# A selective-scan and expert-choice kernel: a reordered prologue, X loaded in one go, and a copy moved to ScalarE

## What is computed

```python
x = x + _layernorm(mamba(_layernorm(x)))
x = x + _layernorm(experts(_layernorm(x)))
# mamba: u, z = split(x @ in_proj);  u = silu(conv1d(u) + conv_b)
#   delta, b, c = split(u @ x_proj);  delta = softplus(delta @ dt_proj + dt_b)
#   h = exp(delta * a) * h + delta * b * u  over 256 steps, 256 channels x 16 states
#   y = (einsum(h, c) + u * D) * silu(z);  return y @ out_proj
# experts: scores = softmax(h @ gate_w.T); each of 16 experts takes its 32 best tokens
#   of a sequence, gated MLP (gelu), scattered back; plus a shared gated MLP
```

## Time and profile of the kernel before

| | us |
|---|---|
| median of 3 runs (1392.88 to 1401.41) | 1394.62 |
| the profiled execution | 1400.59 |
| its span, first to last instruction | 1398.9 |
| first product on GpSimd | 63.42 |
| first scan on VectorE | 65.87 |
| last work of the Mamba block | 908.2 |
| expert block, first part | 908.6 to about 1050 |

### The profile page before, as it was taken

One profiled execution on the slowest core, in us unless ns is written; L12 is line 12 of the kernel. 1 busy time (PEld: TensorE's weight loads), 2 busy tenths in 40 slices (PEclk: granted clock), 3 DMA queues, 4 the chain that ended last, 5 costly groups with the idle time before them and its releaser, 6 DMA issues. The chain is left out here.

```text
span 1398.9 us, 15385 instructions
## 1 busy us (share of the span) xinstructions
PE 1094.9 (78%) x4128; PEld 510.1 (36%) x4128; DVE 1103.3 (79%) x1440; ACT 889.4 (64%) x1614; POOL 938.9 (67%) x503
## 2 busy tenths in 40 slices
PE   4667878787777878777777876445998989999796
PEld 2322222222222222222222322133755336666695
DVE  7499999999999999999999999896382962222288
ACT  3567577667667677667667665356332866666796
POOL 0199999999999999999999999722010740000176
PEclk9878899989999899989998898867798999999898
DMA  5745835834834835834834836110000001111013
GB/s 159 152 101 112 183 71 111 182 81 101 182 77 105 182 75 107 182 85 97 182 81 101 183 81 162 41 31 1 1 0 23 1 1 34 44 35 34 12 31 91
DMA packets 48490, 122.87 MB, mean 88 GB/s; under 512 B 5824, under 2 KB 20928, under 8 KB 42304
## 3 DMA queue, kind: packets, MB, share of 16 engines
q1 hardware_dynamic: 46864, 121.01, 39.1%
q10 hardware_dynamic: 1584, 1.36, 0.3%
HBM read 83.55 MB, written 5.24 MB: 63 GB/s over the span
## 5 line engine op out<-in xcount | busy, mean ns | idle before, releaser
L555 POOL TENSOR_TENSOR states<-b_dup,dup 128x1024 f32<-128x1024 f32 x256 | 596.5, 2359 | 63.3 <-DMA dup<-dd 61.7
L648 DVE TENSOR_TENSOR_SCAN da<-da,states 128x1024 f32<-128x1024 f32 x160 | 359.5, 2283 | 38.7 <-ACT da L397 32.6
L397 ACT ACTIVATE da<-dup,decay 128x510 f32<-128x510 f32 x512 | 327.2, 672 | 11.1 <-DVE states L648 11.1
L295 PE MATMUL yp<-states,fold 128*64 128x512 f32 x1024 | 275.4, 664 | 15.6 <-DVE states L574 9.8
L534 POOL TENSOR_TENSOR states<-states,X 128x1024 f32<-128x1024 f32 x96 | 226.1, 2356 | 20.5 <-DVE states L648 20.4
L648 DVE TENSOR_TENSOR_SCAN states<-da,states 128x1024 f32<-128x1024 f32 x96 | 218.7, 2278 | 7.0 <-ACT da L397 7.0
L574 DVE TENSOR_TENSOR states<-da,X 128x1024 f32<-128x1024 f32 x160 | 192.5, 1203 | 0.0
L1664 POOL TENSOR_SCALAR put<-row_t,slot_i,slot_w 128x256 f32<-128x256 f32 x32 | 39.1, 1222 | 193.3 <-POOLq L1368 173.5
L393 ACT ACTIVATE da<-zeros 128x4 f32<-128x4 f32 x177 | 30.5, 173 | 197.2 <-DVE states L574 196.3
L295 PEld LDWEIGHTS yp<-states,fold 128*64 128x64 f32 x1024 | 69.4, 152 | 212.5 <-issue 196.2
L1469 DVE TENSOR_TENSOR hx<-glx,upx 128x512 f32<-128x512 f32 x64 | 41.3, 684 | 126.6 <-ACT glx L1434 118.2
(11 more groups left out here) (185 smaller groups left out, 1779.9 us busy)
## 6 DMA issues: line engine op xcount, KB each, us to landing
b_dup<-bc_rows SPq DMA_DIRECT2D x32, 1024.0 KB, 9.6
dup<-dd SPq DMA_DIRECT2D x128, 256.0 KB, 11.7
X<-bc_rows SPq DMA_DIRECT2D x64, 512.0 KB, 11.5
out<-X SPq DMA_DIRECT2D x3, 1024.0 KB, 5.1
wg<-in_wgT SPq DMA_DIRECT2D x16, 128.0 KB, 2.1
wu<-in_wuT SPq DMA_DIRECT2D x16, 128.0 KB, 2.2
wd<-in_wdT SPq DMA_DIRECT2D x16, 128.0 KB, 2.2
bc_rows<-bcf SPq DMA_DIRECT2D x16, 64.0 KB, 1.6
```

Source lines behind the costliest of these rows:

```text
L295: last = nc.tensor.matmul(yp[64 * i:64 * i + 64, :], fold[:], states[:, (2 * step + i) % RING, s, :], start=False, stop=(q == 3 and s == S ...
L397: ins = nc.scalar.activation(factors[:, s, :].rearrange("p (b t) -> p b t", b=2)[:, :, 1:S], src[:, :, 1:S], ACT.Exp, scale=decay[:, col:c ...
L555: nc.gpsimd.tensor_tensor(states[:, i % RING], b_dup[:, par, s0:s0 + SPI, :], dup[:, par, 1, h, g, :].unsqueeze(1).broadcast_to([P, SPI, N ...
L648: nc.vector.tensor_tensor_scan(to.rearrange("p s t -> p (s t)"), factors.rearrange("p s t -> p (s t)"), ring.rearrange("p s t -> p (s t)") ...
```

## The change

- SP asks for X in four parts of 4, 28, 16 and 16 tiles (`X_PARTS`), all at the start, without the wait for the weights. ScalarE issues `conv_w` first, and loads its tables ahead of their use (`preload_act_table_set`, `preload_act_table`).
- Only pair 0 goes through statistics, `inverse` and `norm` before the first projection. Pair 1 follows inside the softplus, the others behind it. The statistics of tiles 32 to 47 and 48 to 63 move behind the softplus' last VectorE step.
- The first nine projections alternate between two PSUM banks (`bank`): one waits for the evacuation of the last but one. `wp` moves ahead of CONV0, BC ahead of DELTA0. The softplus of pair 0 runs by channel halves (`log_half`, `lost_half`, `softplus_half`, `inputs_half`), and `whole_banks` fills its two PSUM banks with a matmul at the start.
- The norms of pairs 12 to 15 are done by ScalarE (`normalised`, with `shift` = -mean * rstd).
- In pair 0 SP sends both halves of delta and delta * u before c; GpSimd starts only when VectorE has done all its norms (`xh_ready` 48).
- `take_logits` is done by ScalarE, the first copy at n = 8 behind `turned`, the second at the end.

```diff
+        X_PARTS = ((0, CH), (CH, 2 * QT), (2 * QT, 3 * QT), (3 * QT, TILES))
-        BEFORE = (CONV0, CONV1, DELTA0, DELTA1, BC, Z0, Z1)
+        BEFORE = (CONV0, CONV1, BC, DELTA0, DELTA1, Z0, Z1)
+        def bank(no):
+            return yp if isinstance(no, int) and no < len(BEFORE) + 2 and no % 2 else mp
...
-                if not (isinstance(no, int) and no == 0):
+                if not (isinstance(no, int) and no < len(BEFORE) + 2):
                     pe.wait_ge(mp_free, no)
+                elif no > 1:
+                    pe.wait_ge(mp_free, no - 1)
... TensorE
             pe.wait_ge(id_ready, 1)
-            turn(0)
+            whole_banks(SOFT_FIRST)
+            turn(0, 1)
             pe.wait_ge(w_loaded, SMALL)
+            ... (the four products of wp, from below)
             pe.wait_ge(wc_ready, 1)
             pe.wait_ge(pads_ready, 2)
             pe.wait_ge(tp_free, 1)
             project(CONV0, 0, 0, before(CONV0))
+            pe.wait_ge(wd_ready, 1)
             project(CONV1, 0, 0, before(CONV1))
+            pe.wait_ge(silu_done, 1)
+            project(BC, 0, 0, before(BC))
             project(DELTA0, 0, 0, before(DELTA0))
             project(DELTA1, 0, 0, before(DELTA1))
-            project(BC, 0, 0, before(BC))
             pe.wait_ge(skip_ready, H2 + 2)
-            softplus(0)
-            turn(1)
+            softplus_half(0, lost_first, sum_first)
+            turn(1, 2)
+            softplus_half(1, sp_lost, sp_sum)
             project(Z0, 0, 0, before(Z0))
-            turn(2)
             project(Z1, 0, 0, before(Z1))
-            turn(3)
-            for no, stage in enumerate((CONV0, CONV1)):
-                project(stage, 1, 1, len(BEFORE) + no)
+            turn(2, QP)
+            project(CONV0, 1, 1, len(BEFORE))
+            turn(QP, 2 * QP)
+            project(CONV1, 1, 1, len(BEFORE) + 1)
+            turn(2 * QP, PAIRS)
... ScalarE
+            def log_half(h, exp, one, log):
+                act.wait_ge(mp_free, before(DELTA0) + h + 1)
+                nc.scalar.activation(absx[:, h], absx[:, h], ACT.Exp, scale=-1.0).then_inc(exp, 1)
+                act.wait_ge(exp, 1)
+                nc.scalar.activation(soft(0)[:, h], absx[:, h], ACT.Identity, bias=1.0).then_inc(one, 1)
+                act.wait_ge(one, 1)
+                nc.scalar.activation(logx[:, h], soft(0)[:, h], ACT.Ln).then_inc(log, 1)
+            def normalised(n):
+                act.wait_ge(shift_ready, 1)
+                act.wait_ge(tp_ready, n - 3)
+                for c in range(CH):
+                    t = CH * n + c
+                    ins = nc.scalar.activation(xh[:, n % 4, c, :], X[:, t, :], ACT.Identity, scale=rstd[:, t:t + 1],
+                                               bias=shift[:, t - 3 * QT:t - 3 * QT + 1])
+                ins.then_inc(xh_act, 1)
             act.wait_ge(eps_ready, 1)
-            inverse(0, 0, QT)
+            inverse(0, 0, CH)
             act.wait_ge(decay_ready, 1)
             nc.scalar.activation(decay[:], decay[:], ACT.Exp).then_inc(exp_ready, 1)
-            turned(0)
+            turned(0, 1)
+            nc.scalar.preload_act_table(ACT.Silu)
+            ... (w_delta from wp, from below; CONV0, CONV1, silu as before)
             nc.scalar.preload_act_table_set(LOG_EXP)
-            inverse(1, QT, TILES)
+            parts(0, 0, 0, before(BC))
             evacuate(DELTA0, 0, 0, before(DELTA0))
+            log_half(0, exp_first, one_first, log_first)
             evacuate(DELTA1, 0, 0, before(DELTA1))
-            negative_exp(0, before(DELTA1)); log(0); parts(...); softplus(0); turned(1)
+            log_half(1, sp_exp, sp_one, sp_log)
+            inverse(1, CH, 2 * QT)
+            softplus_half(0, sum_first, delta_first)
+            turned(1, 2)
+            softplus_half(1, sp_sum, delta_ready)
             evacuate(Z0, 0, 0, before(Z0))
-            turned(2)
             evacuate(Z1, 0, 0, before(Z1))
-            turned(3)
+            turned(2, QP)
             evacuate(CONV0, 1, 1, len(BEFORE))
+            turned(QP, 2 * QP)
+            inverse(2, 2 * QT, TILES)
+            turned(2 * QP, 3 * QP - 2)
+            for n in range(3 * QP, PAIRS):
+                normalised(n)
+                turned(n - 2, n - 1)
+            turned(PAIRS - 2, PAIRS)
... GpSimd, item 0 of pair 0
+                            pool.wait_ge(xh_ready, 3 * QT)
... VectorE (w_conv also moves ahead of the steps on w_out)
             dve.wait_ge(x_in[0], 16)
-            statistics(0, QT)
+            statistics(0, CH)
+            dve.wait_ge(rstd_ready, 1)
+            norm(0, 1)
             dve.wait_ge(w_loaded, SMALL)
...
+            statistics(*X_PARTS[1])
+            lost_half(0, log_first, lost_first)
             dve.wait_ge(rstd_ready, 2)
-            norm(1)
-            lost(0)
-            inputs(0, 0)
-            norm(2)
-            norm(3)
+            norm(1, 2)
+            lost_half(1, sp_log, sp_lost)
+            dve.wait_ge(x_in[2], 16)
+            statistics(*X_PARTS[2])
+            inputs_half(0, delta_first, du_first)
+            inputs_half(1, delta_ready, du_ready)
+            norm(2, QP)
+            norm(QP, 2 * QP)
+            dve.wait_ge(x_in[3], 16)
+            statistics(*X_PARTS[3])
+            dve.wait_ge(rstd_ready, 3)
+            nc.vector.scalar_tensor_tensor(shift[:], mv[:, 3 * QT:, 0], -1.0, rstd[:, 3 * QT:], ALU.mult, ALU.mult)
+            norm(2 * QP, 3 * QP)
... SP
-            for i in range(4):
-                if i == 1:
-                    sp.wait_ge(w_loaded, SMALL)
-                sp.dma_start(X[:, i * QT:(i + 1) * QT, :], x_v[:, i * QT:(i + 1) * QT, :]).then_inc(x_in[i], 16)
+            for i, (t0, t1) in enumerate(X_PARTS):
+                sp.dma_start(X[:, t0:t1, :], x_v[:, t0:t1, :]).then_inc(x_in[i], 16)
... experts, ScalarE (the same two calls go from VectorE)
+                def take_logits(half):
+                    act.wait_ge(lp_ready, LP * (half + 1))
+                    nc.scalar.activation(L[:, CH * LP * half:CH * LP * (half + 1), :], lp[:]..., ACT.Copy).then_inc(lp_free, 1)
+                    if n == LP:
+                        take_logits(0)
+                take_logits(1)
```

## The result

The changed kernel takes 1400.95 us (median of 20 runs, 1398.69 to 1403.11), the kernel before beside it 1394.59 (20 runs, 1392.64 to 1401.41): a ratio of 1.0042, interval 1.0035 to 1.0050. That is 6.4 us more and within 1%, as forecast (1399.0). The times of before fall in two groups, near 1394 and near 1402, and its profiled execution (1400.59) is one of the longer; after's profiled execution is 1402.28 (span 1400.6), so the two traces are compared stage by stage and not by their totals.

What follows compares the result with a forecast made beforehand. The loop was taken as bound by VectorE and ScalarE, its start by ScalarE: 17.5 + 51.2 + 1.8 = 70.5, a shift of +5.75, with -1.6 for the logits +4.15. Against the median 1394.62 that gave 1399, range 1388 to 1408.

Steps and rivals of the forecast that it cites:

- The ring: Mamba loop: VectorE, ScalarE, VectorE wait on each other in turn and bound the loop, with GpSimd close behind.
- T: ScalarE's start on pair 0, claimed to set the loop's start: 63.70 before, forecast 70.5, break-even 64.75.
- 0.34 + 0.71: Start of the loop: ScalarE's wait for CONV1's matmuls (0.34) and the seventh scan's wait for factors (0.71), both expected saved.
- w: Prologue: arrival of the ten small weights beside X, taken as 17.5 between ends of 10.6 (undisturbed) and 20.5.
- f: Prologue: time lost to a lower TensorE clock, ahead of BC or in wp and CONV0; 0 to 3.5, taken 1.8, one fall.
- L: Prologue: end of the lost bits of half 1 in pair 0's softplus, put at w + 21.5.
- From L to T, 29.7: Prologue behind the softplus: VectorE's statistics, inputs and norms 19.6, ScalarE's four pairs 8.5, last three copies 1.6.
- The shift, 5.75: Start of the loop: T forecast at 70.5 against the break-even of 64.75, so the loop moves 5.75 later.
- The logits, -1.6: Expert block: ScalarE's copy lets the MLP's down product come 1.85 earlier; 1.6 taken off, ends 0 and 3.5.
- the early weights: Rival in the prologue: w stays 10.6, no clock fall, T 61.8, time 1388 with up to -3.5 from the logits; chance 0.2.
- The slower rival: Prologue: X goes ahead of the weights, clock falls twice; w 20.5, f 3.5, T 75.2, no logits gain, 1405; chance 0.2.
- GpSimd did not set the loop: Rival at the loop's start: GpSimd's start counts, not ScalarE's, 61.7 against 63.42, time 1391; chance 0.1.

Runs made afterwards that it cites:

- before again: The kernel before, unchanged, profiled in a second execution to see where its two groups of times part: 1394.87 us.
- after again: The changed kernel, with no further edit, profiled in a second execution: 1399.73 us.
- before's third execution: The kernel before, unchanged, profiled once more for the groups of times and the spread of the loop's start: 1393.85 us.

## Why the prediction was right

The forecast of 1399.0 was 1.95 short, in the right case and inside its range. Its steps:

- **What bounds, and that the start of the loop decides:** right. The ring of the earlier trace rows is unchanged and ScalarE sets T as said. The loop ends 844.9 to 846.3 behind T in the four executions of before's prologue (T 63.70, 64.45, 60.33, 65.91) and 843.0 to 843.8 in the four of after's (73.25, 73.30, 72.02, 72.16). So the loop moves with T, and what the change saves behind T is about 2, where the prediction has 0.34 + 0.71.
- **w, 17.5 taken, 19.66 measured:** the largest miss, 2.2. The failed step is "nearer to the row, but part of the way back". The upper end (20.5) was near the truth, though not by its reason: the queues share one to one while both are full, and then the last weight is left to trickle. Nor does 20.5 come out of its own numbers: the 5.55 MB of weights and X at 0.29 MB in a microsecond, from 2.5 on, end at 21.6, near where X's packets did end. Moved behind the weights again, X gives 10.6 back.
- **f, 1.8 taken:** L is w + 24.24, so 2.7 above the 21.5 of the working. The 21.5 holds but for its first two terms: from w to the end of CONV1 it took 9.98 in place of 7.2, and from there to L 14.26 in place of 14.3. It was to be one fall out of two, and it is the other one: there was none ahead of BC (BC 1.90 at 31.50), but wp took 3.78 in place of 1.89, and CONV0 behind it 3.80 in place of 2.79, at a granted clock of 0.50 (last of the windows of after below). The 1.9 that the prediction gave this fall was short of the 2.8 that it cost.
- **From L to T, 29.7:** 29.35 measured. ScalarE's norms at 0.40 a tile, as the earlier trace rows gave, are 0.41. GpSimd's new wait costs nothing of its own, as costed: it stands still for scan 1 at 79.29.
- **The shift, 5.75:** 8.4 at the loop's end in the profiled pair, 2.65 more than forecast; the three terms above, 2.2 + 0.9 - 0.35, are that difference. But single executions of one prologue differ: the four of before's prologue in the table end the loop at 908.94 on average (906.63 to 910.92), the four of after's at 915.97 (915.06 to 917.03): 7.0.
- **The logits, -1.6:** near in the stages, undersized in the medians. In the two stages ahead of the softmax the copy costs 0.5 and saves 1.5 against a short execution of before, so -1.0; against the long one it saves 6.5. The medians say -2.8 on before, and -2.1 against its shorter group. "It will still run at the lower clock" is right for the down product (3.79 at 990.27), but it is not the end of the matter: what counts is how soon the clock comes back, which differs by execution, and with the copy on ScalarE the long case did not occur.
- **The sum:** between the two executions near their medians, before again and after again, it is +7.02 for the loop's end, +0.49, -1.45 and -1.96 for the three stages behind, +4.10 of span (1393.1 to 1397.2). Their times are 4.86 apart, since 1.8 stands around the one span and 2.5 around the other. The forecast was +4.15, and the medians give +6.4, so that +4.10 comes so near is luck. That 1399.0 came within 1.95 is luck in part: the shift and, by the medians, the logits were both taken too small, and they have opposite signs. And the -1.96 of the last stage can't be put down to the copy alone: with VectorE's copy put back that stage stays at 383.4. Why before has 385 there is not settled.
- **The rivals:** the early weights did not come (w is not 10.6). The slower rival, with w 20.5 and two falls, was nearest in its first half, but its "nothing from the logits" is refuted. GpSimd did not set the loop.
- **Its signs:** w was to stand at 16 to 19 and L at 39 to 42, and both came later (19.66, 43.90), T too (about 70, 73.25); the norms at 0.4, the two waits and the logits of pair 8 came as said.

## What to carry to other kernels

A bulk load that is issued "as early as possible" delays the small loads that everything waits for, the last of them most: let it wait for them if the first use of the bulk is later anyway. Before work is moved to an engine because it is idle, find which queue sets the stage's end; here the helper's norms lengthened it by 3.4. When a kernel's times fall in groups, look for a long wait of TensorE in the trace, and compare executions of either group stage by stage.

## What the runs showed of the hardware that was not expected

- The last transfer of the small queue got far less than its one-to-one share beside the big one (23 packets to 142): dskip's 1 KB took 12.7 from issue to landing beside X, 5.3 without most of it; with dskip first, `decay` was the one that came last, at 19.27.
- TensorE's first work runs at half pace even where the granted clock reads 1.00: four matmuls of 512 columns took 3.62 at 1.58, 0.90 each, against 2.79 for six, and wp 3.21 in a window that shows 1.00. The Trainium skill (TensorE: Matmul & The Clock Gate, Part 1) says that the lower level is the state in which the engine starts; the paces agree, the clock's column does not show it. In after the windows from 8 us on show the lower level too, 1.2 GHz, after TensorE had stood idle since 5.2:

```profile
0.00:8.00 8.00, 3.62 (x4) 1.18 (x4) 1.21 (x9) 0.57 (x1) 0.84 (x9) 1.00 0.71 207
8.00:10.00 2.00, 0.00 (x0) 0.00 (x0) 0.71 (x3) 1.21 (x3) 0.00 (x0) 0.58 1.04 318
...
12.00:20.00 8.00, 0.32 (x1) 0.32 (x2) 0.34 (x2) 0.12 (x1) 0.00 (x0) 0.50 1.08 290
...
22.00:24.00 2.00, 2.00 (x5) 1.33 (x4) 2.00 (x13) 0.53 (x2) 0.00 (x0) 0.50 0.00 1
```

- One and the same prologue does not take one and the same time. In before's third execution DELTA0 took 1.98, where it took 3.59 at the lower clock, and ScalarE started on pair 0 at 60.33 in place of 63.70:

```profile
30.78 1.98 PE L264 MATMUL mp<-uz,w_delta 128*128 128x512 f32 x4 [1.90 <-ACT w_delta L467]
...
60.33 0.17 ACT L393 ACTIVATE da<-zeros 128x4 f32<-128x4 f32 x1
```
